# Attention steps of 256 rows in an adaLN block, with SyncE's first loads, stores and rows of maxima alternating, later h2 and router stages, and GpSimd squares in the last unit

## What is computed

```python
x = L0_attn_x                                    # (2, 1024, 128)
mod = (_silu(L0_c) @ L0_wmod).reshape(2, 6, 1, -1)
sa, ca, ga, sb, cb, gb = (mod[:, i] for i in range(6))   # gates held at |g| >= 0.25
h = _layernorm(x) * (1 + ca) + sa
# attention: q, k, v = h @ qkv_w + qkv_b, 16 heads; q, k rotated; causal softmax; @ v; @ out_w + out_b
x = x + ga * attention(h)
h = _layernorm(x) * (1 + cb) + sb
# router: expert = argmax(softmax(h @ w_router.T)); f = h @ w_fc[expert].T
# f = where(f >= 0, f, 0.5 f) ** 2 ; out = f @ w_proj[expert].T
x = x + gb * experts(h)
```

## Time and profile before

| | |
|---|---|
| median of three runs | 378.39 us |
| the profiled execution, its own time | 379.6 us |
| its span in the trace | 377.8 us |
| TensorE busy | 348.4 us (92%) |
| VectorE busy | 258.1 us (68%) |
| ScalarE busy | 211.1 us (56%) |
| GpSimd busy | 99.3 us (26%) |
| mean granted TensorE clock | 0.964 of 2.4 GHz |

### The profile page before, as it was taken

The page is one execution under the profiler, slowest core; times in us unless marked ns, Lnnn a source line. Parts: engine busy times, 40 slices in busy tenths (PEclk is TensorE's granted clock), DMA queues, the critical chain, the costliest instruction groups (busy, mean ns, idle before and its releaser), DMA issues.

```text
span 377.8 us, 6872 instructions
## 1 busy us (share of the span) xinstructions
PE 348.4 (92%) x2348; PEld 163.0 (43%) x2348; DVE 258.1 (68%) x561; ACT 211.1 (56%) x407; POOL 99.3 (26%) x183
## 2 busy tenths in 40 slices
PE   6979889999898999999999989999999999989886
PEld 4435454434443333445433433444434445335544
DVE  4935877986996977587778774686887777222254
ACT  5340246743255656775576654854777666694343
POOL 3450633435410424400403011201114133312110
PEclk9996899999898999999999997999999999998999
DMA  7447512222210002340230400400000000000000
GB/s 203 172 133 181 119 45 66 67 64 62 62 53 0 3 1 71 81 89 0 82 74 19 111 0 0 131 0 29 1 2 1 5 3 2 3 0 3 28 2 28
DMA packets 13314, 18.87 MB, mean 50 GB/s; under 512 B 4192, under 2 KB 9184, under 8 KB 13280
## 3 DMA queue, kind: packets, MB, share of 16 engines
q1 hardware_dynamic: 12992, 18.04, 18.2%
q10 hardware_dynamic: 288, 0.39, 0.3%
HBM read 12.98 MB, written 5.24 MB: 48 GB/s over the span
## 4 chain that ended last, share of the span: by engine, by line
PE 73%; DVE 10%; issue 6%; ACT 4%; DMA 3%; POOL 2%; SPq 2%; POOLq 0%; ACTq 0%; DVEq 0%
PE ps_o L1045 18%; PE ps L1008 16%; PE ps L1025 14%; PE ps L979 4%; PE ps L1003 4%; PE ps L966 4%; DVE tmax L843 3%; PE ps L987 3%; PE ps L915 3%; DVE rot L748 2%; ACT pt L648 1%; PE ps L954 1%; PE ps L972 1%; DMA qparts<-part 1%; SPq L434 1%
## 5 line engine op out<-in xcount | busy, mean ns | idle before, releaser
L843 DVE TENSOR_REDUCE tmax<-ps 128x1 f32<-128x512 f32 (+3 forms) x304 | 187.5, 656 | 70.9 <-PE ps L1008 69.9
L648 ACT ACTIVATE pt<-ps 128x512 f32<-128x512 f32 (+1 forms) x304 | 161.6, 574 | 108.4 <-PE ps L1025 106.8
L1008 PE MATMUL ps<-kst,qst 72*128 72x128 bf16 (+3 forms) x576 | 116.8, 281 | 0.6 <-DVE y L826 0.3
L1025 PE MATMUL ps<-qst,kst 75*128 75x512 bf16 (+3 forms) x384 | 112.0, 330 | 4.5 <-DVE rot L748 1.8
L1045 PE MATMUL ps_o<-pt,v_sb 128*32 128x512 f32 (+3 forms) x768 | 83.9, 509 | 3.0 <-POOL pt L543 1.8
L1008 PEld LDWEIGHTS ps<-kst,qst 72*128 72x128 bf16 x576 | 51.0, 101 | 69.4 <-ACT pt L648 18.8
L543 POOL TENSOR_SCALAR_AFFINE_SELECT pt<-pt 128x512 f32<-128x512 f32 x64 | 40.3, 640 | 74.3 <-ACT pt L648 74.0
L1025 PEld LDWEIGHTS ps<-qst,kst 75*128 75x128 bf16 x384 | 35.0, 98 | 30.0 <-issue 8.4
L987 PE MATMUL ps<-maska,identb 128*128 128x512 bf16 x112 | 35.2, 417 | 3.3 <-POOL maska L475 3.3
L513 POOL CAST negp<-negm 128x16 bf16<-128x16 f32 x16 | 3.2, 198 | 103.3 <-DVE negm L769 103.1
L1045 PEld LDWEIGHTS ps_o<-pt,v_sb 128*32 128x32 f32 x768 | 15.5, 108 | 34.1 <-issue 16.6
(11 more groups left out here) (99 smaller groups left out, 254.3 us busy)
## 6 DMA issues: line engine op xcount, KB each, us to landing
qst<-qparts SPq DMA_DIRECT2D x48, 96.0 KB
kst<-kparts SPq DMA_DIRECT2D x48, 96.0 KB
qparts<-part SPq DMA_DIRECT2D x16, 96.0 KB, 1.9
kparts<-part SPq DMA_DIRECT2D x16, 96.0 KB, 1.9
xs<-in_x SPq DMA_DIRECT2D x4, 256.0 KB, 7.2
rope_sb<-in_rope SPq DMA_DIRECT2D x2, 512.0 KB, 6.2
qparts<-part SPq DMA_DIRECT2D x16, 64.0 KB, 1.8
qst<-negt SPq DMA_DIRECT2D x48, 4.0 KB, 1.7
```

The lines of the kernel that those rows point to most:

```text
L648: act.activation(pt[:, G % NP, h0:h0 + nh, 0:w], src, ACT.Exp, scale=SCALE).then_inc(s_exp, 1)
L843: dve.tensor_reduce(dst, src, AX.X, ALU.max).then_inc(s_max, 1)
L1008: last = pe.matmul(dst[:, j * nk:(j + 1) * nk], qst[0:ROWS, half, h, r * P:r * P + P], kst[0:ROWS, kh, h, k0:k0 + nk], start=(kind != "dia ...
L1025: last = pe.matmul(dst[:, j * w:(j + 1) * w], kst[:, kh, h, kt * P:kt * P + P], qst[:, half, h, c0:HALF], start=True, stop=True)
```

## The change

A step now has 256 query rows of a unit (`qh` is 0 or 1), so there are 32 steps. Pass A has the same 304 banks in the same order. Pass B works on pairs of key tiles, each tile with 256 query columns; the second tile of a diagonal pair has 128. A step of half 0 has 3 or 7 banks of pass B, one of half 1 has 11 or 15: 288 in all, every one 512 columns wide, with the same number of columns in sum. The product with v is issued for a pair, 80 pairs (160 tiles) where 96 tiles were. The matmuls of pass B are 640 where 384 were, the transposes of maxima 64 in 32 stages where 16 in 16 were. `LEAD` and the lag of the product with v stay 8 and 3 slots.

Beside it: SyncE's stores and loads of unit (0,0) alternate by group of heads, the loads of groups 2 and 3 moving behind slots 7 and 16; 12 filler matmuls stand ahead of the first bank of pass A; the row of FIXED moves q2 to k3 of unit (0,1) by 1 to 3 slots; for the units of b = 0, h2 and rt stand 2 slots later each, and for (0,0) also a1 to a3, ohT, m0 and m1; in the last unit, ohT stands ahead of a1, and GpSimd squares c = 1 and 3 of each piece.

By the lists of the two plans: before, slots 0 to 18 and 63 to 78 have no bank of pass B (35 slots), and 35 banks of pass B stand behind slot 303. Now 0 to 10, 14 to 18, 29, 40, 51, 59 to 62, 74 to 78, 105, 132, 159, 186, 213, 240 and 267 have none (35 slots), and 19 banks stand behind slot 303. Ahead of slot 79 stood steps 0 to 3 of pass B (four groups of heads of unit (0,0)); now there also stand the 11 banks of step 8, the first of unit (0,1), with three pairs of products.

```diff
-STEPS = [(b, half, g) for b, half in UNITS for g in range(NG)]
+STEPS = [(b, half, g, qh) for b, half in UNITS for g in range(NG) for qh in range(2)]
-def groups_b(half):
-    out = []
-    if half:
-        out += [(kt, 0, 0, [(h, 1) for h in range(HG)]) for kt in range(TU)]
-    for kt in range(TU):
-        n = HALF - kt * P
-        nh = max(1, HALF // n) if n < 384 else 1
-        out.append((kt, half, kt * P, [(h, nh) for h in range(0, HG, nh)]))
+def groups_b(half, qh):
+    pairs = [(kh, kt) for kh in range(half + 1) for kt in range(0, TU if kh < half else TQ * (qh + 1), 2)]
+    out = []
+    for kh, kt in pairs:
+        diagonal = (kh, kt) == (half, TQ * qh)
+        out.append([(kt, kh, 0, [(0, 2), (2, 2)]),
+                    (kt + 1, kh, P, [(0, 4)]) if diagonal else (kt + 1, kh, 0, [(0, 2), (2, 2)])])
-FIXED = {("q1", (0, 1)): 3, ("q2", (0, 1)): 6, ("q3", (0, 1)): 8, ("k1", (0, 1)): 12, ("k2", (0, 1)): 15, ("k3", (0, 1)): 18}
+FIXED = {("q1", (0, 1)): 3, ("q2", (0, 1)): 7, ("q3", (0, 1)): 9, ("k1", (0, 1)): 15, ("k2", (0, 1)): 18, ("k3", (0, 1)): 21}
-WARM_PRE = {"start": 7, "mod": 4, "hT": 4, "v": 44}
+WARM_PRE = {"first": 12, "start": 7, "mod": 4, "hT": 4, "v": 44}
-    + [("load", (0, 0), g) for g in range(NG)] + [(name, (0, 1)) for name in ["norm1", "var1", "nz"]] \
+    + [("load", (0, 0), g) for g in range(2)] + [(name, (0, 1)) for name in ["norm1", "var1", "nz"]] \
-        put(a_end[s] + MAX_LAG, "max2", s)
+        put(a_end[s] + (MAX_LAG + 2 if s in (0, 1) else MAX_LAG), "max2", s)
+    for g, at in ((2, 7), (3, 16)):
+        put(at, "load", (0, 0), g)
-                at = max(at + POST[name], POST_AT.get((name, (b, half)), 0))
+                at = max(at + POST[name] + (b == 0) * {"h2": 2, "rt": 2}.get(name, 0)
+                         + (b == half == 0) * {"a1": 2, "ohT": 1, "a2": 2, "a3": 2, "m0": 1, "m1": 1}.get(name, 0),
+                         POST_AT.get((name, (b, half)), 0))
-                    if st[1:] == ((0, 0), 0):
+                    if st[1] == (0, 0) and st[2] < NG - 1:
                         for i in range(2):
-                            store((0, 0), i, range(1, NG))
+                            store((0, 0), i, [st[2] + 1])
+                if name[0] == "a" and (u, int(name[1])) in squares_pool:
+                    c, (t0, t1) = int(name[1]), tiles(u)
+                    wait_read(pool, name, u)
+                    f = fg[:, c, P * t0:P * t1]
+                    pool.tensor_tensor(f, f, f, ALU.mult).then_inc(s_fsp, 1)
-                pe.transpose(dst[0:PARTS * HG * TU, 0:P // 2].bitcast(BF16),
-                             negp[:, s % 2].rearrange("p c m -> p (c m)"), identb[:, :]).then_inc(full_, 1)
+                for r in range(TQ):
+                    last = pe.transpose(rows[:, P * r:P * r + P],
+                                        negp[:, s % 2, r].rearrange("p c h -> p (c h)"), identb[:, :])
```

More of the change, by code:

```diff
@@ L56, with bank_jobs_a @@
 PIECES[UNITS[-1]] = [(0, TU // 2), (TU // 2, TU)]
-STEPS = [(b, half, g) for b, half in UNITS for g in range(NG)]
-def bank_jobs_a(half):
+QW = HALF // 2
+TQ = TU // 2
+STEPS = [(b, half, g, qh) for b, half in UNITS for g in range(NG) for qh in range(2)]
+STEP_NO = {step: s for s, step in enumerate(STEPS)}
+def bank_jobs_a(half, qh):
     jobs = []
-    for r in range(TU):
+    for r in range(TQ * qh, TQ * qh + TQ):
         jobs.append(("diag", r, 0, HG, P))
@@ L128, in plan @@
     slot, v_end = 0, []
-    for s, (b, half, g) in enumerate(STEPS):
+    for s, (b, half, g, qh) in enumerate(STEPS):
         slot = max(slot, a_end[s] + LEAD)
-        for gi, grp in enumerate(groups_b(half)):
-            for bank in grp[3]:
-                b_at[slot] = (s, gi, grp, bank, bank is grp[3][-1])
-                slot += 1
-            v_at[slot - 1 + PVLAG] = (s, gi, grp)
+        for gi, pair in enumerate(groups_b(half, qh)):
+            for j, tile in enumerate(pair):
+                for bank in tile[3]:
+                    b_at[slot] = (s, gi, j, tile, bank, bank is tile[3][-1])
+                    slot += 1
+            v_at[slot - 1 + PVLAG] = (s, gi, pair)
         v_end.append(slot - 1 + PVLAG)
@@ L320, in adaln_block @@
         s_xb, s_fs, s_out = sem("s_xb"), sem("s_fs"), sem("s_out")
-        squares = []
+        s_fsp = sem("s_fsp")
+        squares, squares_pool = [], [(u, c) for c in (1, 3) for u in
+                                     [UNITS[-1] + (k,) for k in range(len(PIECES[UNITS[-1]]))]]
         block = ctx.enter_context(nc.Block())
@@ L588, in run @@
                     if n:
-                        for which in range(2):
-                            stored(act, i, n, which)
+                        stored(act, i, n)
                     act.activation(part[i][:, 0], full[i][:, :], ACT.Copy).then_inc(s_part[i], 1)
```

167 lines of the change are left out of this document (89 added, 78 removed).

## The result

The changed kernel took 386.19 us (median of 4 runs, 384.16 to 390.2) beside 379.07 us for the kernel before on the same chip: 1.022 of the time before, with a 95% interval of 1.015 to 1.028. It is slower, by 1.5 to 2.8%; the prediction was 373.5 us, and its range ended at 381.

A forecast was written before the change was run, and what follows sets the result against it. TensorE was taken as the bound, busy 348.4 of 377.8 us, solid from 261.4 to 282.2. Terms 1.0 + 4.1 + 1.5 - 5.0 + 0 - 6.5 + 1.0 - 1.0 + 0 = -4.9 us gave 373.5 us against the median; range 366 to 381.

The forecast's parts named there:

- The start: Up to slot 19: fillers gain 3 us, a 3 to 4 us wait follows; taken as 0, ends -2 and +3.
- the new first pass B waits for SyncE: Start: SyncE's stores and loads run to 37.1, so pass B begins at about 40.2 us.
- h2 and rt later: Units of b = 0: later stages remove TensorE's waits and slow clock, -6.5 us; -1.5 if the wait moves.
- SyncE at slot 138: Step 14's rows of maxima stand behind 4 stores and 12 loads: +1 us, ends 0 and +3.
- Stalls only move: Rival: stalls of h2 and rt move to ohT or a later wait, -1.5 for -6.5, 378.5 us; chance 0.11.
- Products: Products with v, 80 pairs for 96 tiles, 0.06 us a seam: +1.0 us, ends -4 and +15.
- Narrow matmuls: Pass B: 256 more matmuls cost 0; rival, they wait for weights, +7 us, 380.5 us, chance 0.04.
- Maxima: Behind slot 79, 22 max2 stages of 0.32 us stand for 11 of 0.27: +4.1 us.
- Moved work: 5.6 us of work moved ahead of slot 79, absorbed in 88.0 to 102.2: -5.0 us, between -5.6 and -1.
- Seven late fillers: Seven of 35 empty slots now lie behind slot 79, where TensorE is the bound: +1.5 us.
- Fillers at the start: 12 fillers fill 2.62 us of waiting; the clock stays up and the 6.6 us to 34.3 shrink by 3.
- Tail: 7 product groups where 14 stood at the end: -1.0 us; the last unit's edits together 0.

The follow-up runs named there:

- experiment 10: Experiment 7's kernel without the added slots of the expert stages of (0,0), h2 and rt still late: ratio 0.990 (0.984 to 0.996), median 377.55.
- experiment 9: The changed kernel without the added slots of the expert stages of (0,0), h2 and rt still late: ratio 1.012 (1.004 to 1.020).
- experiment 7: The changed kernel with stores of (0,0) first again and first rows of maxima ahead of the third group's loads: 1.000 (0.994 to 1.007), median 384.07.
- experiment 14: The kernel before with the 12 filler matmuls ahead of its first bank of pass A, nothing else: ratio 1.001 (0.995 to 1.007).
- experiment 13: Experiment 7's kernel without any added slots of later stages, without the 12 fillers, last unit as before the change: 1.002 (0.997 to 1.008), median 377.98.
- experiment 1: The changed kernel with maxima of step 0 ahead of q2 on ScalarE, SyncE's order kept: ratio 1.011 (0.995 to 1.026), median 385.56.
- experiment 2: The changed kernel with the first rows of maxima ahead of the third group's loads, max2 of step 0 in slot 6: 1.010 (1.005 to 1.015).
- experiment 3: The changed kernel with the first loads of b = 1 moved from slot 138 to behind step 14's rows: ratio 1.009 (1.004 to 1.015).
- experiment 6: Experiment 2's kernel with a buffer of its own for q of unit (0,1), so q2 waits for no store: 1.013 (1.005 to 1.021).
- experiment 15: Experiment 7's kernel without added slots of later stages, stores of q of (0,1) behind the second step's rows: ratio 1.004 (0.999 to 1.009).

## Why the prediction was wrong

**The start** (taken at 0, ends -2 and +3). The step that failed is "the new first pass B waits for SyncE". SyncE's queue was reckoned rightly: its stores were out at 40.2 instead of 37.1, 2.5 us of this from the late start of that execution. But I followed the rows of maxima through SyncE's list alone. They pass ScalarE's too, and there q2 of the next unit waits for every store of this one. The change puts the last stores behind two more groups' loads; who waits for a store's landing was never asked. The wait was 7.92 us instead of 3 to 4, and slot 19 came 26.0 us behind slot 0 where it had been 19.3 and 18.3: the term measured +6.7 to +7.7 instead of 0. The fillers in it gave 1.7 to 2.6 us by slot 5 (6.0 against 7.7 and 8.6), not 3. Undoing the order of the stores alone took 4.9 us off in the trace and brought the ratio to 1.000. A full price of this mechanism (+5 to +8) would have been the rival on the other side.

**h2 and rt later** (-6.5). On the kernel before all lags together are worth 4.4 to 7.6 us in the trace up to slot 206 and 2.7 (ratio) to 4.2 us (median) in the time. Late h2 and rt alone, on steps of 256 rows, brought 0.8 to 2.0 us in slots 79 to 148 and nothing in the time (experiment 10). The step that failed in the changed kernel is that I gave the term no cost. It wasn't one edit: the expert stages went with it, and they were the cover of another term.

**SyncE at slot 138** (+1, "with that cover doubled it would be 0, with k3 2 us later +3"). Measured 2.90 us of wait, at the upper end, and half clock from 181.9 to 188.7 us, some 3 us that the sum had not. The cover that I listed (ohT, v, a2, a3) is right for the changed plan; I never compared it with before, where m0 to y0 stood there too. Without the expert lags the stretch of slots 79 to 160 is 4.5 us shorter (experiment 9), and with the start repaired 10 (experiments 7 and 10: 93.0 and 82.8, with 17 us of half clock in the first); the time differs there by 3.8 (ratio) to 6.5 us (median).

**Stalls only move** was the rival that came true for (0,1): the waits of 0.86 and 0.92 us around h2 and rt are gone, and 0.95 and 0.90 us stand elsewhere. It had 0.11 and deserved more. That steps of 256 rows have twice as many points at which pass B can wait is a reason I give, not one that a run shows.

**Products** (+1.0). Mis-sized on the safe side: a pair of two full tiles takes 285.53 - 284.52 = 1.01 us, with 0.09 ahead of it, about what one tile of 512 took (0.99 and 0.10). The seam costs nothing that can be seen, so the term is the lower end, 80 x 0.24 - 96 x 0.24 = -3.8 us. This agrees with the Trainium skill (TensorEngine Tiling (Array Packing), Key Properties), by which a change of tiling mode drains TensorE: both tiles of a pair have one mode.

**Narrow matmuls** (0) was right. A bank of four 128-column matmuls or two of 256 takes 0.22 us here as before. The 81 ns a matmul of the Trainium skill (TensorE: Matmul & The Clock Gate, Back-to-back issue gap) would make 0.32 of it; the trace disagrees.

**Maxima** (+4.1): a stage's two transposes take 115.22 - 115.01 = 0.21 us, and 115.01 - 114.69 - 0.22 = 0.10 ahead of them where nothing waits, as taken. Other stages behind slot 79 wait another 0.3 us and more for GpSimd's `negp` (0.31 at 283.78), which the sum had not.

```profile
114.69 0.38 PE L1050 MATMUL ps<-qst,kst 75*128 75x256 bf16 x2
115.01 0.28 PE L950 MATMUL ps<-identb,negp 128*12 128x128 bf16 x2
115.22 0.39 PE L1033 MATMUL ps<-kst,qst 72*128 72x512 bf16 x1
```

**Moved work** (-5.0): slots 63 to 79 take 13.8 us with it, as forecast. **Seven late fillers** (+1.5) weren't measured apart. **Fillers at the start**: the clock holds, as forecast, and it brings nothing by slot 30 (experiment 14). **Tail** (-1 and 0): 1.6 to 3.3 us for the last unit's edits in the traces of experiment 13, more than I took, and 0.8 in the medians.

So the terms behind slot 79 sum to about what was said (4.6 to 5.6 us less in the trace, for 4.9). That is luck in part: products and tail came out better than taken, h2 and rt and slot 138 worse. The start decided.

What stays open: the traces differ by 2.2 to 2.8 us behind the common start, the medians by 7. Much of this is which runs were traced: the changed kernel's is 2.0 us below its median, and the second trace of before, with the same late start, 2.2 above its own (381.24 and 379.04). That the rest is waits of 1 to 8 us, each of which can bring a stretch of half clock or not, is argued, not shown. Nor is it sure that the loss is the full 2.2%. The changed kernel had four runs, and experiments 1, 2, 3 and 9, which undo quite different things, all lie at 1.009 to 1.012, though behind slot 0 the trace of experiment 9 is only 0.7 us shorter than the changed kernel's.

## What to carry to other kernels

For a transfer that is moved later, look at who waits for it, on every engine, and at what stands behind that wait in the engine's list; the wait for a buffer to be free counts as much as the wait for data. For a stage that is moved later, ask which wait it was covering, also where it seems idle work: its own gain and this cover are one term. And a critical chain through several in-order queues is as late as the latest of them, so that freeing one shows the next (experiments 2, 6 and 15).
